# A four-stage transformer kernel on one core: norms and residuals moved across the two stage changes around layer 1's attention

## The reference

```
layer 0: causal attention, 16 heads of 64
         mixture of 8 routed (top 2) and 2 shared SwiGLU experts, hidden 256
layer 1: h = LN(x)
         h = h + global_latent_attention(rmsnorm(h, norm1_w))
         h = h + local_attention(rmsnorm(h, norm2_w))       # window of 32
         x = x + LN(h)
         x = x + LN(soft_mixture(LN(x)))                    # 8 experts, 64 slots each
soft_mixture(x): xn = rmsnorm(x) * gamma;  sn = rmsnorm(slot_embeds) * slot_gamma
         logits = xn . sn; softmax over tokens dispatches, over slots combines
```

## Time and profile before

| | |
|---|---|
| median of three runs | 2453.27 us (2449.40, 2453.27, 2456.77) |
| profiled execution | 2459.24 us; its span 2457.5 us |
| TensorE busy | 2214.6 us (90%) |
| VectorE busy | 1459.5 us (59%) |
| ScalarE busy | 1229.4 us (50%) |
| GpSimd busy | 1054.8 us (43%) |
| mean granted clock of TensorE | 0.959 |

### The profile page before, as it was taken

How to read it: one execution, slowest core, us unless ns; L and a number is a source line. 1 busy time by engine, 2 the same in 40 slices (tenths; PEclk the granted TensorE clock), 3 DMA queues, 4 the chain that set the end, 5 groups by cost and what they waited for, 6 DMA issues and landing times. The chain is left out here.

```text
span 2457.5 us, 40332 instructions
## 1 busy us (share of the span) xinstructions
PE 2214.6 (90%) x15428; PEld 1400.2 (57%) x15428; DVE 1459.5 (59%) x3240; ACT 1229.4 (50%) x1796; POOL 1054.8 (43%) x980
## 2 busy tenths in 40 slices
PE   4999999999999999985999999489999988876787
PEld 2555565556555565545888888334444455555667
DVE  3677758775777757753666666535545555545533
ACT  2555545554465535541333333167777866644543
POOL 0677757775677757771323223323322311100001
PEclk9999999999999999997999999679999999998999
DMA  2000000000000000002000000000000000003001
GB/s 74 1 1 1 1 1 1 1 1 1 1 1 1 1 1 1 1 1 65 1 1 1 1 1 1 7 1 1 1 1 1 1 1 2 2 3 74 1 1 35
DMA packets 36322, 18.19 MB, mean 7 GB/s; under 512 B 16666, under 2 KB 33956, under 8 KB 36132
## 3 DMA queue, kind: packets, MB, share of 16 engines
q1 hardware_dynamic: 36132, 15.61, 2.5%
HBM read 13.50 MB, written 2.10 MB: 6 GB/s over the span
## 5 line engine op out<-in xcount | busy, mean ns | idle before, releaser
L311 POOL TENSOR_TENSOR a_first<-a_first,a_ring 128x512 f32<-128x512 f32 (+3 forms) x352 | 559.3, 1589 | 142.2 <-ACT a_ring L556 106.9
L1645 ACT ACTIVATE g_probsT<-g_s_ps 128x1024 f32<-128x1024 f32 (+2 forms) x448 | 368.9, 869 | 143.2 <-PE g_s_ps L1514 89.0
L556 ACT ACTIVATE a_ring<-a_st 128x768 f32<-128x768 f32 (+1 forms) x256 | 234.8, 917 | 263.0 <-PE a_st L463 263.0
L478 PE MATMUL a_o_ps<-a_ring,a_v 128*64 128x512 f32 (+3 forms) x1280 | 249.2, 485 | 3.2 <-POOL a_ring L293 2.2
L645 DVE RECIPROCAL a_row_inv<-a_row_inv 128x512 f32<-128x512 f32 x64 | 213.9, 3343 | 16.8 <-ACT a_row_inv L544 16.8
L993 ACT ACTIVATE m_silu<-m_up,m_b 128x512 f32<-128x512 f32 x160 | 110.1, 688 | 220.8 <-PE m_up L927 220.7
L623 DVE TENSOR_REDUCE a_part_max<-a_mx 128x2 f32<-128x1024 f32 x128 | 156.6, 1223 | 103.2 <-PE a_mx L434 100.1
L1545 PE MATMUL g_o_ps<-g_probsT,g_values 128*32 128x512 f32 (+5 forms) x2688 | 213.1, 430 | 5.2 <-POOL g_probsT L1397 5.1
L850 POOL TENSOR_TENSOR m_acc<-m_acc,m_part 128x512 f32<-128x512 f32 x72 | 99.2, 1378 | 271.1 <-DVE m_part L1122 271.1
L1397 POOL TENSOR_SCALAR_AFFINE_SELECT g_probsT<-g_probsT 128x512 f32<-128x512 f32 x128 | 89.0, 698 | 255.2 <-ACT g_probsT L1645 255.0
L1514 PE MATMUL g_s_ps<-g_qT,g_kT 64*128 64x512 f32 (+3 forms) x896 | 173.9, 436 | 27.1 <-ACT g_probsT L1645 21.3
(11 more groups left out here) (287 smaller groups left out, 4373.7 us busy)
## 6 DMA issues: line engine op xcount, KB each, us to landing
m_w<-in_L_ffn_rw SPq DMA_DIRECT2D x2, 1024.0 KB, 8.4
s_w<-in_L_ffn_w SPq DMA_DIRECT2D x1, 2048.0 KB, 10.6
s_w<-in_L_ffn_w SPq DMA_DIRECT2D x4, 512.0 KB, 10.5
out_x<-x SPq DMA_DIRECT2D x8, 256.0 KB, 2.3
m_w<-in_L_ffn_rw SPq DMA_DIRECT2D x2, 512.0 KB, 5.2
x<-in_L_attn_x SPq DMA_DIRECT2D x1, 512.0 KB, 4.3
a_outT<-in_L_attn_w_q SPq DMA_DIRECT2D x1, 512.0 KB, 5.2
a_outT<-in_L_attn_w_k SPq DMA_DIRECT2D x1, 512.0 KB, 6.1
```

The source lines that it names most:

```text
L311: pool.tensor_tensor(total[:, h, q:q + w], total[:, h, q:q + w], probs_of(n, u)[:, h, off:off + w], ALU.add).then_inc(added, 1)
L478: last = pe.matmul(o_ps[rows_of(h), first_q:first_q + w], v_half[n // 4 % 2][:, j, head:head + A_HD], probs_of(n, u)[:, h, off:off + w], s ...
L556: act.activation(probs_of(n, u)[:, :, 0:w], st_ps[u % 2][:, :, 0:w], ACT.Exp).then_inc(exp_done, 1)
L1645: act.activation(out, src.rearrange("p k (j n) -> p k j n", j=at_once), ACT.Exp, scale=float(HD) ** -0.5).then_inc(exp_done, 1)
```

## The change

**At the first seam** the weights and tables of the attention become tiles of the caller (`AttentionWeights`), loaded by the mixture's SP list behind its own loads. In the mixture's last batch VectorE makes the layer norm of batch 0 for the attention (`norms_of_attention`, steps 11 to 16), its square, sum and scale (steps 17 to 19) and the scaling of both input weights (steps 11 and 12). GpSimd has one more power at step 13 and one at 18. The residual of batch 3 leaves the mixture: its sum now lies in `g.hidden`, and the attention works it off in round 0, steps 8 to 14 (`left_over`), with its power at step 10 of GpSimd's list. The preparation no longer has norms; GpSimd zeroes from step 0 on, and ScalarE waits for it at steps 12 and 18.

**At the second seam** SP issues the four small loads of the soft mixture in the attention's list, once round 7's input is turned and round 6's residual is done. In round 7, steps 1 to 13, VectorE makes batch 0's norm and the slots' norm and scaling (`norm_for_mixture`), now with its own `tensor_scalar` in place of ScalarE's `normalize(0)`; GpSimd has powers at steps 3 and 7. The residual of batch 3 leaves the remainder and goes into units 3 to 7 of the soft mixture's batch 0 (`last_residual`). The tiles of these norms lie in freed parts of `g.hidden` and `g.normed`.

The diff, cut to its core:

```diff
@@ mixture_layer0: SP, GpSimd
+                g.weights.load(sp, g, attention_loaded)
...
-                                        or i == NEXT_ROOT_AT and s < M_UNITS - M_WINDOW):
+                                        or i == NEXT_ROOT_AT):
                         inverse_root(pool, norm, g.minus_half[:, 0:NB], roots)
                         roots += 1
-                inverse_root(pool, norm, g.minus_half[:, 0:NB], roots)
+                    if s == M_UNITS - M_WINDOW + RMS_ROOT_AT:
+                        pool.wait_ge(rms_ready, 1)
+                        pool.tensor_tensor(rms_root[:], rms_sum[:], g.minus_half[:, 0:NB], ALU.pow).then_inc(root_ready, 1)
@@ mixture_layer0: VectorE
+                    def square():
+                        chain.settle()
+                        own.did(dve.tensor_tensor(g.normed[:], first, first, ALU.mult))
+                    def sum_up():
+                        own.settle()
+                        own.did(dve.tensor_reduce(rms_sum[:], g.normed[:], AX.X, ALU.add))
+                        own.settle()
+                        dve.tensor_scalar(rms_sum[:], rms_sum[:], 1.0 / D, RMS_EPS, ALU.mult, ALU.add).then_inc(rms_ready, 1)
+                    def scale():
+                        dve.wait_ge(root_ready, 1)
+                        own.did(dve.tensor_tensor(g.normed[:], first, rms_root[:].unsqueeze(2).to_broadcast([P, NB, D]),
+                                                  ALU.mult))
+                    return layernorm_parts(dve, chain, x_of, out_of, norm, norms[0] - 1)[:-1] + [square, sum_up, scale]
...
-                        nexts = norm_of(b + 1) if b + 1 < BATCH else []
+                        nexts = norm_of(b + 1) if b + 1 < BATCH else norms_of_attention()
...
+                    if b + 1 == BATCH:
+                        for k in {17: (7,), 18: (8,), 19: (9,)}.get(i, ()):
+                            nexts[k]()
+                        if i in (11, 12):
+                            scale_weights(i - 11)
                 weigh(M_UNITS - 1)
-                for piece in residual(BATCH - 1):
-                    piece()
@@ layer1_attention: SP
+                for half in range(2):
+                    x_read(sp, "input", ROUNDS - 1, 0, half)
+                sp.wait_ge(norm1.chain, NORMS_TO_SECOND_RESIDUAL)
+                g.soft.load(sp, g, soft_loaded)
@@ layer1_attention: GpSimd
-                        if x < BATCH and n == 2:
-                            inverse_root(pool, norm1, g.minus_half[:, 0:NB], x)
-                            if r < 0:
-                                zero_values()
+                        if x in NORM_COUNT and n == 2:
+                            inverse_root(pool, norm1, g.minus_half[:, 0:NB], NORM_COUNT[x])
+                        if r == 0 and n == 10:
+                            inverse_root(pool, norm1, g.minus_half[:, 0:NB], 1)
+                        if r < 0 and n == 0:
+                            zero_values()
+                            zero_slots()
@@ layer1_attention: ScalarE
-                act.wait_ge(zeroed, 9)
-                act.wait_ge(loaded, LOADS * 16)
...
+                        if r < 0 and n == 12:
+                            act.wait_ge(zeroed, 4)
+                        if r < 0 and n == 18:
+                            act.wait_ge(zeroed, 9)
@@ layer1_attention: VectorE
+                    left_over = residual(BATCH - 1, 1) if r == 0 else []
+                    ends = residual(r - 1, r - 1) if BATCH < r < ROUNDS else []
+                    soft_parts = norm_for_mixture() if r == ROUNDS - 1 else []
...
+                        if soft_parts:
+                            for i in {1: (0,), 2: (1,), 3: (2,), 5: (3,), 6: (4,), 7: (5,), 9: (6,), 10: (7,), 11: (8,),
+                                      12: (9,), 13: (10,)}.get(n, ()):
+                                soft_parts[i]()
+                        if left_over:
+                            for i in {8: (0, 1), 9: (2, 3), 10: (4,), 12: (5,), 13: (6,), 14: (7,)}.get(n, ()):
+                                left_over[i]()
@@ soft_mixture: ScalarE, VectorE
-                normalize(0)
                 keep_input(0)
...
+                    if b == 0:
+                        for k in {3: (0, 1), 4: (2, 3), 5: (4,), 6: (5,), 7: (6, 7)}.get(u, ()):
+                            ends[k]()
```

## The result

The changed kernel took 2416.95 us in the median of four runs (2412.19 to 2418.69), the kernel before 2454.90 beside it; the ratio is 0.9845, with a 95% interval of 0.9825 to 0.9864. A second measurement of the same file beside later experiments gave 2413.38 us against 2456.23, ratio 0.9836 (0.9807 to 0.9865). So the change saves 38 to 43 us. The forecast was 2415.0 us (2404 to 2428), and faster.

A forecast was written before the change was run, and what follows sets the result against it. At the seams a chain of dependent steps, mostly VectorE norms, bounds the kernel; inside stages TensorE mostly sets the pace. Savings of 21.1 and 17.2 us, 38.3 in all, off the 2453.3 median give 2415.0 us (2404 to 2428).

The forecast's parts named there:

- seam 1, start of the first transposes: Between mixture and attention: TensorE's first transposes start at 1551.70 in place of 1571.40, saving 19.7 us.
- ScalarE's wait for the zeroing: Head of the attention's preparation: ScalarE no longer waits there for GpSimd to zero `q_slots`, saving 2.0 us (0 to 2.2).
- mixture's last window: Mixture's last batch: moved norm pieces are covered; square, sum and scale at steps 17 to 19 cost 0.1 us (0 to 1.4).
- residual in round 0: Attention round 0, steps 8 to 14: batch 3's residual, 6.0 us of work, costs 0.5 us (0 to 6.0).
- seam 2, start of the first transposes: Between attention and soft mixture: TensorE starts at 2202.48 in place of 2221.51, saving 19.0 us.
- norm and slots in round 7: Attention round 7: added norm and slot work fits free time; the small loads' wait costs 0.3 us (0 to 3).
- last residual in the soft mixture: Soft mixture, batch 0: residual pieces ahead of VectorE's reductions cost 3.0 us (0 to 6.0).
- clock up at the soft mixture: Start of the soft mixture: TensorE's clock may stay at 2.4 GHz after a short pause, saving 1.5 us (0 to 3.8).
- rival (a): Soft mixture, rounds 0 and 7, first seam: inserted work lies fully on the path, 11.9 us more, 2427 us; chance 0.17.
- rival (b): After both seams the clock stays up: 2.3 us more at the second, about 5 in the preparation, 2408 us; chance 0.17.
- Rival (d): Attention round 0: the clock does not rise after the shorter preparation, some 62 us more, 2477 us; chance 0.03.

The follow-up runs named there:

- the second seam alone: The changed kernel with the mixture-to-attention part put back as in the kernel before, keeping only the attention-to-soft-mixture part: 2435.21 us, ratio 0.9909.
- the first seam alone: The changed kernel with the attention-to-soft-mixture part put back as in the kernel before, keeping only the mixture-to-attention part: 2433.05 us against 2457.81, ratio 0.9906.

## Why the prediction was right

The total came out at 38 to 43 us where the sum said 38.3, and the sum's terms can now be set against measured ones:

| term | forecast | measured |
|---|---|---|
| seam 1, start of the first transposes | 19.7 | 20.0 |
| ScalarE's wait for the zeroing | 2.0 | 2.06 |
| mixture's last window | -0.1 | -0.06 |
| residual in round 0 | -0.5 | -0.1 |
| seam 2, start of the first transposes | 19.0 | 19.03 |
| norm and slots in round 7 | -0.3 | 0.0 |
| last residual in the soft mixture | -3.0 | -1.6 |
| clock up at the soft mixture | +1.5 | +1.5 over the whole stage |
| sum | 38.3 | 40.8 |

The measured terms come to what the three stretches outside the rounds lost in the traces, 41.1 and 40.9 us. All the misses lie on one side, a saving taken too low or a price too high; most of it is the last residual's 1.4 us.

**The two seams.** The reading of the profile on which all rested held: at a seam one chain of norms on VectorE set TensorE's start, and taken out of the way it showed in full. The two stage changes cost 0.35 and 0.32 us where I had 0.54 and 0.32. At seam 1 VectorE's `scale` was started 0.16 us before GpSimd's addition and the pair of additions took 3.58 us instead of twice 1.26; the last one ended 0.53 us later than before, as against 0.65 by the forecast. Moving `scale` a step ahead gave the 0.53 back, so it is shown to come from there. The trace also shows a wait: the addition of the unit before the last began at 1550.33, `scale` ended at 1550.17 + 1.21 = 1551.38, and two additions of 1.26 behind that end at 1553.90, where the pair ended at 1553.91. That is also what the Trainium skill's "SBUF — State Buffer" (Who interferes with whom) would have: the second of the two waits for the first.

**The covered work.** Mixture steps, round 0 and round 7 swallowed their pieces at 0.1 us or less, each shown by a kernel without it: the mixture's steps stayed at 4.55 us, and from the 21st last `weigh` to the last it is 104.93 us before, 104.94 with the second seam alone, and 104.99 in the changed kernel. The rival (a), inserted work in full on the path, fell with them.

**The term that was mis-sized** is the last residual in batch 0 of the soft mixture: I added up 1.0, 1.0, 1.0 by the idle times in the earlier trace rows and got 3.0; it measured 1.6, and which of its pieces cost that stays open. The traces of before and after alone (37.40 to 39.02) gave the same figure by accident, since the clock's gain of 1.6 and a drop of 1.7 cancelled in that stretch; the run without the residual alone would have said 3.3. Only both with the clock beside them gave the price.

**The clock.** The term at the second seam was right in kind: the clock stayed up over TensorE's pause of 1.05 us, where it had fallen in one of 20. That its size came out at the 1.5 of the forecast is luck: I had taken 1.5 of at most 3.8 without a row for it, and it is what 2.6 us and a later drop leave. At the first seam rival (b) had the clock up in the preparation for 5 us more. This came true in some executions only: from ScalarE's first read to the first rotation it is 13.33 us at 0.63 in the changed kernel and before, but 9.74 at 0.94 with the first seam alone:

```profile
1552.60:1562.34 9.74, 8.71 (x40) 5.38 (x38) 0.00 (x1) 4.46 (x12) 5.78 (x9) 0.94 0.00 0
```

Of the ten profiled executions with the first seam's change four had such a shorter stretch (by 2.7 to 3.6 us). It varies with the execution, and is worth more than several terms of my sum; with the drops in the rounds it can account for two medians of one file 3.6 us apart. Rival (d), the clock that doesn't rise in round 0, did not happen: it rose at 1601.3, 9.5 us after the first score (8.4 before), and the 83 us above had a mean of 0.96.

## What to carry to other kernels

Where a stage begins with a chain of norms on one engine, put it into the stage in front in steps where that engine idles: here most of the 28.4 us that VectorE was busy at the two seams went there at a price of some 2.3 us (1.6 for the last residual, 0.5 for the addition that `scale` pushed, 0.2 for the rest), and the waits at the head of the new stage (a zeroing, small loads) have to be moved with it, or they take the place of the norms. Before a difference of 1 or 2 us between two traces is put down to an edit, lay the granted clock of the same stretch beside it, and build the kernel without the edit. A filler on TensorE gained nothing where ScalarE was the bound (7.80 us at 0.56 and at 0.78). In front of the soft mixture it gained 2.6 us up to the first slots' sum and 1.5 over the stage, less than the 7 us by which it overran the gap. Neither made the whole kernel measurably faster.

## What the runs showed that I had not expected

TensorE's clock drops for some 3.4 us at a time in dense stretches too, after 6.67 us of work in 7.00. In the rounds of the attention their places differ between executions of the same program; in the changed soft mixture they stood at the same places in all eight executions. One drop costs 1.2 to 1.7 us where it was measured, and the rounds of the attention held 34 to 56 us at the lower level, and their length went from 581.6 us (34) to 591.5 (55). The wait for the zeroing would have cost 5.4 us in the new arrangement, over twice what it cost before: a wait that is cheap beside slow work gets dear when that work is gone.
